# In the passes over the edges, VectorE's second operands move from SBUF to PSUM and three copies move to ScalarE

## The reference, cut to what matters

```python
x = layernorm(x + L0(x))   # agg = segment_sum(x[src] * norm, dst), then two dense layers
x = layernorm(x + L1(x))   # e = relu(score(src, dst, type)); softmax of e over the edges of dst
                           # segment_sum(alpha * Z[src, type], dst)
x = layernorm(x + L2(x))   # segment_sum(x[src], dst) + (1 + eps) * x, then two dense layers
x = layernorm(x + L3(x))   # 4 heads: leaky_relu(w_k[src] + w_q[dst] + w_e), softmax over dst
                           # segment_sum(hn[src] * attn, dst)
```

## Time and profile before

| What | Value |
| --- | --- |
| Median of 3 runs | 10099.64 us (10096.38 to 10099.9) |
| The profiled execution, its own time | 10036.1 us |
| Its span in the profile | 10034.4 us |
| GpSimd busy | 7578.5 us, 76% |
| VectorE busy | 3383.1 us, 34% |
| ScalarE busy | 1391.9 us, 14% |

### The profile page before, as it was taken

The page is one execution under the profiler, slowest core; times in us unless marked ns, Lnnn a source line. Parts: engine busy times, 40 slices in busy tenths (PEclk is TensorE's granted clock), DMA queues, the critical chain, the costliest instruction groups (busy, mean ns, idle before and its releaser), DMA issues. The chain is left out here.

```text
span 10034.4 us, 21314 instructions
## 1 busy us (share of the span) xinstructions
PE 493.3 (5%) x3908; PEld 414.0 (4%) x3908; DVE 3383.1 (34%) x2929; ACT 1391.9 (14%) x1369; POOL 7578.5 (76%) x6764
## 2 busy tenths in 40 slices
PE   6000000000300000000000000000020000000000
PEld 6000000000200000000000000000020000000000
DVE  7222222222432222222225666666323222222222
ACT  0111111111211111111111111111111111111111
POOL 0777777777677777777767777777767777777776
PEclk9999999999655555555555555555555555555555
DMA  1211111111322121221222222222222212122221
GB/s 58 57 47 44 47 47 47 47 47 46 96 50 47 44 47 44 47 47 44 48 57 72 77 78 79 79 79 79 53 34 69 52 48 52 48 52 48 51 51 43
DMA packets 319095, 553.49 MB, mean 55 GB/s; under 512 B 157061, under 2 KB 164980, under 8 KB 311988
## 3 DMA queue, kind: packets, MB, share of 16 engines
q0 software_dynamic: 216064, 226.41, 12.9%
q1 hardware_dynamic: 102942, 326.10, 8.6%
HBM read 298.89 MB, written 253.15 MB: 55 GB/s over the span
## 5 line engine op out<-in xcount | busy, mean ns | idle before, releaser
L445 POOL DMA_INDIRECT rows_a<-table,idx_c_a x3224 | 3750.7, 1163 | 982.5 <-issue 982.5
L445 POOL DMA_INDIRECT rows_l<-table,idx_c_l x3224 | 3519.3, 1092 | 1229.3 <-issue 981.9
L862 DVE TENSOR_TENSOR score_a<-rows_a,target_a 128x26 f32<-128x26 f32 (+1 forms) x124 | 34.2, 276 | 3317.0 <-DMA rows_a<-table,idx_c_a 3317.0
L650 DVE COPY msg_l<-rows_l 128x1664 f32<-128x1664 f32 x124 | 197.2, 1591 | 2721.2 <-DMA rows_l<-table,idx_c_l 2721.2
L797 ACT COPY back_a<-msg_a 128x1690 f32<-128x1690 f32 (+1 forms) x124 | 416.7, 3361 | 516.0 <-DVE msg_a L902 516.0
L545 ACT COPY back_l<-msg_l 128x1664 f32<-128x1664 f32 x124 | 384.6, 3102 | 701.3 <-DVE msg_l L658 701.3
L787 ACT ACTIVATE diff_a<-diff_a 128x52 f32<-128x52 f32 (+1 forms) x124 | 38.6, 311 | 3171.0 <-DVE diff_a L879 3171.0
L436 ACT COPY idx_c_l<-src_i 128x26 int32<-128x26 int32 x124 | 25.8, 213 | 3263.0 <-DVE msg_l L650 3238.9
L902 DVE TENSOR_TENSOR_SCAN msg_a<-keeps_a,msg_a 128x1690 f32<-128x1690 f32 (+1 forms) x124 | 466.3, 3760 | 24.9 <-DVE msg_a L897 24.8
L658 DVE TENSOR_TENSOR_SCAN msg_l<-keeps_l,msg_l 128x1664 f32<-128x1664 bf16 x124 | 451.9, 3644 | 4.5
L419 DVE TENSOR_REDUCE part<-prod_e 125x132 f32<-125x8448 f32 x50 | 447.6, 8953 | 1.7
(11 more groups left out here) (228 smaller groups left out, 1721.3 us busy)
## 6 DMA issues: line engine op xcount, KB each, us to landing
prefix<-back_l SPq DMA_DIRECT2D x124, 832.0 KB, 3.6
prefix<-back_a SPq DMA_DIRECT2D x62, 936.0 KB, 3.7
prefix<-back_a SPq DMA_DIRECT2D x62, 858.0 KB, 3.5
rows_l<-table,idx_c_l POOLq DMA_INDIRECT x3224, 2.5
rows_a<-table,idx_c_a POOLq DMA_INDIRECT x3224, 2.5
feat<-edge_attr SPq DMA_DIRECT2D x50, 1031.2 KB
table<-stage SPq DMA_DIRECT2D x49, 260.0 KB, 2.1
spread<-zero SPq DMA_DIRECT2D x12, 806.0 KB
```

Of the source, the lines that this page charges most:

```text
L445: pool.indirect_dma_start(rows[:, s * CH + k, 0:row], None, table, bass.IndirectOffsetOnAxis(idx_c[:, s, k:k + 1], 0))\
L650: nc.vector.tensor_copy(msg[:, u], rows[:, s * CH:(s + 1) * CH, :].rearrange("p k f -> p f k")).then_inc(taken, 1)
```

## The change

- `keeps` moves to PSUM as one f32 buffer in both kinds of pass, and gets one column more for each feature. `msg` gets a column 0 that holds the carry from the chunk before. The scan runs over 27 columns for each feature where it ran over 26, and the separate carry steps (lines 654, 894 and 897) and `same0` are gone; ScalarE copies the carry column.
- `gather_sum`: ScalarE, and no longer VectorE, copies the gathered rows into `msg`, and that copy now releases the list of chunk c + 4. In L0 ScalarE writes the target's halves, one chunk at a time, into PSUM as f32, and VectorE compares the SBUF iota with them.
- `attend`: score, running maximum, differences and probabilities lie in PSUM; ScalarE copies the score out of the slot; the exponential is taken in two instructions; `best` is copied back to SBUF for each chunk; in A3 the leaky curve is a product and a maximum where it was one instruction.
- In both, ScalarE's copy back of chunk c - 1 now stands in its queue ahead of its work on chunk c. Small PSUM tiles of the pass ends share a bank.

```diff
@@ one_hots @@
-                nc.vector.tensor_tensor(hot[:, s], iota_h[:, 0:n], part[:, c * CH:(c + 1) * CH].unsqueeze(1).broadcast_to([P, n, CH]),
+                nc.vector.tensor_tensor(hot[:, s], iota_h[:, 0:n], part.unsqueeze(1).broadcast_to([P, n, CH]),
@@ gather_sum @@
-                msg = tsb(f"msg_{tag}", [P, 2, D, CH])
-                keeps = tsb(f"keeps_{tag}", [P, 2, D, CH], BF16)
+                msg = tsb(f"msg_{tag}", [P, 2, D, 1 + CH])
+                keeps = tps(f"keeps_{tag}", [P, D, 1 + CH])
...
+                        def halve(c):
+                            for n, part in enumerate((part_i, shift_i)):
+                                nc.scalar.copy(half_ps[c % HSLOTS][:, n], part[:, c * CH:(c + 1) * CH]).then_inc(halves, 1)
...
                         for c in range(CHUNKS):
-                            u = c % 2
+                            s, u = c % SLOTS, c % 2
+                            if c:
+                                act.wait_ge(scanned, c)
+                            nc.scalar.copy(keeps[:, :, 1:1 + CH], same16[:, c * CH:(c + 1) * CH].unsqueeze(1).broadcast_to([P, D, CH]))\
+                                .then_inc(keeps_ready, 1)
+                            if c:
+                                nc.scalar.copy(msg[:, u, :, 0:1], msg[:, 1 - u, :, CH:1 + CH]).then_inc(carried, 1)
+                                keep_back(c - 1)
+                            if first and c + HSLOTS < CHUNKS:
+                                act.wait_ge(hot_ready, 2 * (c + 1))
+                                halve(c + HSLOTS)
+                            act.wait_ge(gathered[s], 16 * CH * (c // SLOTS + 1))
+                            if c >= 2:
+                                act.wait_ge(back_ready, c - 1)
+                            nc.scalar.copy(msg[:, u, :, 1:1 + CH], rows[:, s * CH:(s + 1) * CH, :].rearrange("p k f -> p f k")).then_inc(taken, 1)
                             if c + SLOTS < CHUNKS:
                                 lists(act, idx_c, src_i, taken, chunk_ready, c + SLOTS)
...
-                            dve.wait_ge(gathered[s], 16 * CH * (c // SLOTS + 1))
-                            nc.vector.tensor_copy(msg[:, u], rows[:, s * CH:(s + 1) * CH, :].rearrange("p k f -> p f k")).then_inc(taken, 1)
-                                link(nc.vector.scalar_tensor_tensor(msg[:, u, :, 0], msg[:, 1 - u, :, CH - 1], same0[:, c:c + 1], msg[:, u, :, 0],
-                                                                    ALU.mult, ALU.add))
...
-                            nc.vector.tensor_tensor_scan(flat, keeps[:, u].rearrange("p f k -> p (f k)"), flat, 0.0, ALU.mult, ALU.add)\
+                            nc.vector.tensor_tensor_scan(flat, keeps[:].rearrange("p f k -> p (f k)"), flat, 0.0, ALU.mult, ALU.add)\
@@ attend @@
+                            if c:
+                                keep_back(c - 1)
+                                nc.scalar.copy(msg[:, u, :, 0:1], msg[:, 1 - u, :, CH:1 + CH]).then_inc(carried, 1)
+                                act.wait_ge(diff_ready, c)
+                            act.wait_ge(gathered[s], 16 * CH * (c // SLOTS + 1))
+                            nc.scalar.copy(score, rows[:, s * CH:(s + 1) * CH, score_at:score_at + heads].rearrange("p k h -> p h k")).then_inc(score_in, 1)
                             act.wait_ge(diff_ready, c + 1)
-                            nc.scalar.activation(diff[:, u], diff[:, u], ACT.Exp).then_inc(exp_ready, 1)
+                            nc.scalar.activation(prob, diff[:, 0:heads], ACT.Exp).then_inc(exp_ready, 1)
+                            nc.scalar.activation(fall[:], diff[:, heads:2 * heads], ACT.Exp).then_inc(exp_ready, 1)
...
-                            link(nc.vector.tensor_tensor(score[:], fetched[:, :, score_at:score_at + heads].rearrange("p k h -> p h k"), target[:, :, here], ALU.add))
+                            link(nc.vector.tensor_tensor(score, score, target[:, :, here], ALU.add))
...
-                            link(curve(score[:]))
+                            if edge_scores:
+                                link(nc.vector.tensor_scalar(slope[:], score, 0.01, None, ALU.mult))
+                                link(nc.vector.tensor_tensor(score, score, slope[:], ALU.max))
+                            else:
+                                link(nc.vector.tensor_scalar(score, score, 0.0, None, ALU.max))
...
+                            link(nc.vector.tensor_copy(best[:, u], best_ps))
...
-                                nc.vector.tensor_tensor(msg[:, u, 0:D], fetched[:, :, 0:D].rearrange("p k f -> p f k"), prob.broadcast_to([P, D, CH]), ALU.mult)\
+                                nc.vector.tensor_tensor(msg[:, u, 0:D, 1:1 + CH], fetched[:, :, 0:D].rearrange("p k f -> p f k"), prob.broadcast_to([P, D, CH]),
...
-                                link(nc.vector.tensor_tensor(by_head(hold[:]), by_head(msg[:, 1 - u, :, CH - 1]),
-                                                             diff[:, u, heads:2 * heads, 0:1].broadcast_to([P, heads, part]), ALU.mult))
-                                link(nc.vector.tensor_tensor(msg[:, u, :, 0], msg[:, u, :, 0], hold[:], ALU.add))
...
-                            nc.vector.tensor_tensor_scan(flat, keeps[:, u].rearrange("p f k -> p (f k)"), flat, 0.0, ALU.mult, ALU.add)\
+                            nc.vector.tensor_tensor_scan(flat, keeps[:].rearrange("p f k -> p (f k)"), flat, 0.0, ALU.mult, ALU.add)\
```

More of the change, by code:

```diff
@@ L530, in _ @@
                         if first:
-                            act.wait_ge(parts, 1)
-                            nc.scalar.copy(lo16[:], part_i[:]).then_inc(halves, 1)
-                            nc.scalar.copy(hi16[:], shift_i[:]).then_inc(halves, 1)
+                            act.wait_ge(parts, 2)
+                            for c in range(HSLOTS):
+                                halve(c)
                             act.wait_ge(masks_ready, 1)
-                        act.wait_ge(keeps_clear, 1)
@@ L548, in _ @@
+                        keep_back(CHUNKS - 1)
                         if first:
@@ new lines, in keep_back @@
+                        def keep_back(c):
+                            u = c % 2
+                            if c >= 2:
+                                act.wait_ge(stored[u], 16 * (c // 2))
+                            act.wait_ge(scanned, c + 1)
+                            nc.scalar.copy(back[:, u, :, sums:wide].rearrange("p k h -> p h k"), best[:, u, :, 1:1 + CH]).then_inc(back_ready, 1)
+                            nc.scalar.copy(back[:, u, :, 0:sums].rearrange("p k f -> p f k"), msg[:, u, :, 1:1 + CH]).then_inc(back_ready, 1)
@@ L844, in _ @@
                         link = linked(dve, chain)
-                        nc.vector.memset(best[:, 0, :, 0:1], 0.0).then_inc(one, 1)
-                        nc.vector.memset(keeps[:, :, :, 0:1], 0.0).then_inc(keeps_clear, 1)
+                        nc.vector.memset(best_ps[:, :, 0:1], 0.0).then_inc(one, 1)
+                        nc.vector.memset(keeps[:, :, 0:1], 0.0).then_inc(clear, 1)
+                        nc.vector.memset(msg[:, 0, :, 0:1], 0.0).then_inc(clear, 1)
                         link(nc.vector.memset(into_t[:, 0:1], 0.0))
@@ L867, in _ @@
+                            for h in range(heads):
+                                last = nc.vector.tensor_tensor_scan(best_ps[:, h, 1:1 + CH], mneg16[:, here], score[:, h], best_ps[:, h, 0:1], ALU.add, ALU.max)
+                                chain.on(last)
+                            dve.wait_ge(chain.sem, chain.n)
                             if c >= 2:
                                 dve.wait_ge(back_ready, 2 * (c - 1))
-                            if c:
-                                link(nc.vector.tensor_copy(best[:, u, :, 0:1], best[:, 1 - u, :, CH:CH + 1]))
@@ L871, in _ @@
-                            for h in range(heads):
-                                last = nc.vector.tensor_tensor_scan(best[:, u, h, 1:1 + CH], mneg16[:, here], score[:, h], best[:, u, h, 0:1], ALU.add, ALU.max)
-                                chain.on(last)
-                            dve.wait_ge(chain.sem, chain.n)
-                            nc.vector.tensor_tensor(diff[:, u, 0:heads], score[:], best[:, u, :, 1:1 + CH], ALU.subtract)\
-                                .then_inc(chain.sem, 1)
```

169 lines of the change are left out of this document (88 added, 81 removed).

## The result

The changed kernel took 9976.89 us (median of 4 runs, 9974.65 to 9981.54), the kernel before 10099.77 beside it: 0.9879 of it, 95% interval 0.9862 to 0.9896. That is 1.2% less, beyond the interval but too little to be called faster by a bar of 2%, and far from the 8950 us forecast. Measured again later, the same changed kernel took 8881.62 us against 10048.02, a ratio of 0.884 (0.8825 to 0.8854). Both results stand; most of what follows is on why they differ. The second came late, so the experiments are told in the order in which they were run. The letter in a run's name is its session: the runs with one letter were made together on one chip, with the kernel before beside them.

What follows compares the result with a forecast made beforehand. GpSimd's gather issue was taken to bound the kernel, lengthened by holds from two-SBUF-operand VectorE instructions. 10036.1 - 1153.7 (holds) + 4 (tails) = 8886.4 us, plus 63.5 for timed runs: 8950 us, ratio 0.886, range 8920 to 9115.

Steps and rivals of the forecast that it cites:

- The holds: In all four passes, VectorE instructions with two SBUF tensor operands hold GpSimd's gathers; 1153.7 us, all to vanish.
- The tails and gaps: Serial work behind each pass's last gather grows: +1.3 us each in L0, L2, +0.8 in A1, A3; +4 us in all.
- Scan, multiply and one-hots at no hold: With one operand in PSUM these VectorE instructions leave no hold on gathers; L0's one-hots lengthen from 1.88 to about 3.5 us.
- Rivals 1 and 2: 1 (chance 0.06): scans go on holding, 685 us, total 9635; 2 (0.03): only the copy's move helps, 157 us, total 9947.
- ScalarE's copy: In L0 and L2 the row copy of line 650, moved to ScalarE, takes 3.10 us and holds no gather.
- The cover: VectorE and ScalarE stay under 32.5 us a chunk, and lists have 97 us of lead, so work behind gathers stays hidden.
- rival 3: GpSimd starves for lists behind ScalarE's queue, decisive from 37.2 us a chunk upwards; +1760 us, total 11860; chance 0.03.
- The sum for a profiled execution: Whole kernel: 10036.1 us less 1153.7 of holds plus 4 of tails gives 8886.4 us.
- What would show it: Signs: gathers below 1.1 us, mean 0.95, 32.5 us a chunk, GpSimd busy near 6430 us, its waits only issue.
- A pass lasts as long as its 1612 gathers take to issue: In all four passes gather issue sets the time, plus a short tail; a plain chunk would need 32.5 us.
- 63.5: Microseconds by which the timed median, 10099.64, exceeded the profiled execution, 10036.1; added to 8886.4 to give 8950 us.
- The range: Up to 9115 us if one multiply holds on in one pass; down to 8920 by smaller offset, tails and gather times.

Runs made afterwards that it cites:

- m1: The changed kernel itself, not altered, measured again in a later session: 8881.62 us, 0.884 of the kernel before.
- p1: The kernel before, not altered, measured again in another session: 10156.73 us.
- f3: Changed kernel with nothing computed on L2's rows and L0's counting behind its loop, plus a one-column GpSimd memset behind each L2 gather: L2 took 2263.3 us.
- f4: Changed kernel with nothing computed on L2's rows and L0's counting behind its loop, plus 50 one-column VectorE memsets per L2 chunk: 10419.63 us, L2's gathers 2231.8.
- m2: Changed kernel with L0's counts from SBUF as before and VectorE copying the rows in L0 and L2: 9058.78 us, 0.9018 of the kernel before.
- k1: Changed kernel with nothing computed on L2's rows, L0's counting behind its loop, and L2's gathers cut to 8 of 128 partitions: 8879.2 us.
- f1: Changed kernel with nothing computed on L2's rows, L0's counting behind its loop, and L2's gathers cut to 64 of 128 partitions: L2 took 2230.3 us.

## Why the prediction was wrong, and where it was right

- **The holds** (1153.7 us, all to vanish): right. From before to m1 the passes lost 249.9, 327.2, 209.7 and 359.2 us, 1146.0 in all; the sum had 249.9, 330.2, 211.3 and 362.3. The tails and gaps grew by 2 us where it had 4.
- **Scan, multiply and one-hots at no hold**: right. In m1 GpSimd's mean gather is 0.95 us in all passes (1531.35 / 1612). The one-hots with the PSUM operand take 3.62 us (estimate 3.5). Rivals 1 and 2 are out.
- **ScalarE's copy**: 3.0 us against 3.10, and it holds no gather.
- **The cover**: there in m1, where no gather inside a pass waits for a list. In the first measurement it failed in L0, by the way of rival 3: ScalarE's queue, but with TensorE as the late one, which the rival didn't name. It didn't decide from 37.2 us a chunk upwards, as the rival said, but from the matmuls' own pace.
- **The sum for a profiled execution**: 8886.4 us; m1's own profiled execution took 8893.18. **What would show it** named GpSimd busy near 6430 (6432.0), mean 0.95 and only issue in its waits within the passes: all seen, in m1. The longest gather falls below 1.1 us only behind the first four chunks of each pass; the 40 longer ones stand in those.
- **The step that failed**, for the result of 9976.89, is that the 1153.7 us of holds come off the time in full: "A pass lasts as long as its 1612 gathers take to issue", at "26 x (0.944 + 0.305) = 32.5 us" a chunk. I took it for granted that gathers can go on at this pace; in the trace of before no chunk had (the shortest took 34.9 us). Under the cap it holds up to the seventh to tenth chunk of a pass; afterwards it is 36.4. The passes could win 127 us (A1) and 151 us (A3) down to 2229, nothing in L2, and L0 lost 117. That is 161 us in place of 1153.7; the gaps between the passes and the end grew by 101 in place of 4, so the profiled execution fell by 60, and the timed runs, which for the kernel before had the cap already, by 123.
- **A second step failed**, and it decides m1: "The median of the runs, 10099.64, stands 63.5 above that execution's own 10036.1; I add the same". I took a difference of conditions for a constant. p1 shows what it was: an unchanged kernel took 10156.73 us, with landing times missing as under the cap, where the profile that I read was taken without it. The three runs shown agreed within 4 us, so an execution 60 us below them could not be one of theirs. In the first result this error was luck: the changed kernel's profiled execution (9976.4) stood at its median, and without the 63.5 the forecast would have been further off.
- The range (8920 to 9115) misses both results, the first by 862 us and m1's by 38: without the cap the 63.5 us should not have been there at all, and 8886 would have been the forecast.

**What stays open** is what the cap is. Measured: it spares the first seven to ten chunks of a pass, during which GpSimd gets 13 to 23 gathers ahead of one in 1.40 us; its settled pace counts none of rows, bytes, GpSimd's memsets, VectorE's or SyncE's instructions, while the free start is shorter with GpSimd's memsets (f3); while gathers run it paces TensorE, VectorE and SyncE in steps of 0.70 and 1.40 us an instruction, after a first burst of 22 on VectorE; and where it stands, records of landings and of releases are missing from the trace. That fits a way for records of the profile that drains too slowly in some sessions and holds back whoever writes into it. The Trainium skill, page "NOTIFIC — the notification-queue block", sections "7.1 Overflow: three behaviours, one of which stalls the engine" and "10. Constraints, capacities, measured rates", says that the internal pipeline of these records holds its producers back rather than lose one, and that about 500 are in flight; an estimate from that page: 500 over a lead of 13 to 23 gathers would be 22 to 38 records for each. It also says that writing a record costs an engine nothing, which f4 would contradict if this is the way. Every run here was made with its cores' spans recorded, so none can show what the kernel takes when nothing is recorded. The cause is argued, not shown.

## What to carry to other kernels

Compare the profiled execution with the timed runs before building on it. If it stands far outside their spread, as here by 60 us beside 4, suspect another condition, and don't add the difference as a constant. Undoing a hold is worth something only as far as the next limit: read from the start of a pass whether a pace lasts, for here seven to ten chunks ran free before the cap closed. And when a variant is as slow as the full kernel with nearly all its work taken out, leave the kernel alone and repeat an unchanged one in another session.

## What I had not expected of the hardware

- The same kernel at 9976.89 and 8881.62 us, each within 0.15% in its own session, while the kernel before moved by 0.5 to 1.3% only (10029.52 and 10048.02 against 10099.77 to 10156.73). A change can be worth 1.2% or 11.6% by the condition that it is measured in.
- A memset of 0.06 us on VectorE, with nothing to wait for, coming once in 1.40 us; a matmul pair of 0.1 us coming once in 2.8.
- One-hots with a PSUM operand take 3.62 us where they take 1.88 from SBUF, and hold no gather; with both in SBUF, and the copy back on VectorE, L0 is 127 us longer (m2 against m1).
- A gather of 8 rows takes 0.85 us of GpSimd, one of 64 rows 0.90 and one of 128 rows 0.94 (k1, f1, m1): nearly all of it is for the instruction, not for the rows.
